# Routed experts: 48-row pieces of two tiles' down projections side by side on halves of TensorE's array, their weights fetched for each tile

## What is computed

```python
logits = jnp.einsum('ed,btd->bte', gate_w, x)
scores = jax.nn.sigmoid(logits) + gate_b
weights, indices = jax.lax.top_k(scores, TOP_K)
weights = weights / weights.sum(-1, keepdims=True)
shared_out = jax.nn.silu(x @ w1_shared) * (x @ w3_shared) @ w2_shared
...
h1 = jnp.einsum('btd,edc->btec', x, w1_routed)
h2 = jnp.einsum('btd,edc->btec', x, w3_routed)
h3 = jax.nn.silu(h1 * h2)
experts_out = jnp.einsum('btec,ecd->bted', h3, w2_routed)
routed_out = jnp.einsum('bted,bte->btd', experts_out, router_probs)
return shared_out + routed_out
```

## Time and profile before

| | |
|---|---|
| median of 3 runs | 1259.91 us (1259.74 to 1263.67) |
| the profiled execution's own time | 1262.89 us |
| its span | 1261.1 us |
| PE busy | 1217.7 us (97%), 10122 matmul records |
| PEld busy | 1072.9 us (85%) |
| DVE, ACT, POOL busy | 848.5, 602.7, 499.1 us (67, 48, 40%) |
| DMA | 111.29 MB, 88 GB/s over the span |
| chain that ended last | PE 87%, DVE 7%, issue 2%, DMA 2%, ACT 1%, POOL 1% |
| L816, PE, up projection | x316, 469 ns each |
| L833, PE, routed down projection | x316, 380 ns each |

### The profile page before, as it was taken

The page is one execution under the profiler, slowest core; times in us unless marked ns, Lnnn a source line. Parts: engine busy times, 40 slices in busy tenths (PEclk is TensorE's granted clock), DMA queues, the critical chain, the costliest instruction groups (busy, mean ns, idle before and its releaser), DMA issues.

```text
span 1261.1 us, 26966 instructions
## 1 busy us (share of the span) xinstructions
PE 1217.7 (97%) x10122; PEld 1072.9 (85%) x10122; DVE 848.5 (67%) x1706; ACT 602.7 (48%) x1353; POOL 499.1 (40%) x489
## 2 busy tenths in 40 slices
PE   5999999999998999999989999999999999999997
PEld 4788888888887777777779999999999999999996
DVE  5646776676677444344458878787886766777686
ACT  3434434433443455555545455454555545555543
POOL 2121433433424300000057767767764444444443
PEclk9999999999999999999999999999999999999999
DMA  6764325415129433333221201101110100000001
GB/s 221 287 227 160 125 74 189 156 48 185 52 77 360 157 106 105 105 102 109 80 101 30 63 26 60 34 27 59 33 61 1 34 1 1 1 2 1 1 26 43
DMA packets 62847, 111.29 MB, mean 88 GB/s; under 512 B 6912, under 2 KB 35456, under 8 KB 61184
## 3 DMA queue, kind: packets, MB, share of 16 engines
q1 hardware_dynamic: 56576, 92.77, 20.9%
q0 software_dynamic: 6144, 16.79, 4.2%
HBM read 49.37 MB, written 60.16 MB: 87 GB/s over the span
## 4 chain that ended last, share of the span: by engine, by line
PE 87%; DVE 7%; issue 2%; DMA 2%; ACT 1%; POOL 1%; SPq 0%; POOLq 0%; DVEq 0%
PE bank L816 8%; PE six L833 6%; PE bank L895 4%; PE bank L893 4%; PE bank L894 4%; PE six L934 4%; PE bank L430 4%; PE bank L432 3%; PE bank L431 3%; PE bank L971 2%; PE bank L969 2%; PE bank L970 2%; PE bank L906 2%; PE bank L905 2%; PE bank L907 2%; PE six L935 2%
## 5 line engine op out<-in xcount | busy, mean ns | idle before, releaser
L1817 DVE TENSOR_TENSOR sq<-xs 128x512 f32<-128x512 f32 x128 | 131.0, 1024 | 39.3 <-ACT xs L1312 39.3
L2037 POOL TENSOR_TENSOR rstd<-msq,half_pow 128x8 f32<-128x8 f32 x64 | 106.0, 1657 | 95.7 <-DVE msq L1824 93.9
L1293 ACT ACTIVATE pT<-six,rstd 128x256 f32<-128x256 f32 x128 | 60.8, 475 | 169.0 <-PE six L935 169.0
L2049 POOL TENSOR_TENSOR pT<-pT,tri_mul 128x512 f32<-128x512 f32 x64 | 82.0, 1281 | 142.6 <-ACT pT L1341 142.6
L816 PE MATMUL bank<-experts,xT 128*128 x316 | 109.5, 469 | 0.8 <-ACT xT L1237 0.8
L1964 POOL TENSOR_TENSOR hid_l<-hid,hid_h 128x256 fp32r<-128x256 f32 x64 | 48.4, 757 | 147.3 <-ACT hid_h L1070 147.2
L893 PE MATMUL bank<-bw_h,xT1h 128*128 128x512 f32 x256 | 105.6, 413 | 0.8 <-ACT v L1317 0.8
L1381 DVE TENSOR_TENSOR yT1l<-six,yT1h 128x512 fp32r<-128x512 f32 x64 | 44.3, 692 | 84.6 <-ACT yT1h L1346 84.6
L895 PE MATMUL bank<-bw_l,xT1h 128*128 128x512 f32 x256 | 100.3, 392 | 0.0
L894 PE MATMUL bank<-bw_h,xT1l 128*128 128x512 f32 x256 | 100.0, 390 | 0.0
L2040 POOL TENSOR_TENSOR qn<-xs,rstd 128x256 f32<-128x256 f32 x128 | 91.6, 737 | 5.0
(11 more groups left out here) (295 smaller groups left out, 3913.5 us busy)
## 6 DMA issues: line engine op xcount, KB each, us to landing
cells_scratch<-zeros SPq DMA_DIRECT2D x8, 4352.0 KB
xg<-cells_scratch SPq DMA_DIRECT2D x79, 128.0 KB, 2.1
cells_scratch<-y SPq DMA_DIRECT2D x79, 128.0 KB, 1.7
experts<-pack_experts_dram SPq DMA_DIRECT2D x16, 608.0 KB
raw<-pack_attn_dram SPq DMA_DIRECT2D x8, 1024.0 KB, 5.0
w_full<-pack_w_dram SPq DMA_DIRECT2D x2, 1024.0 KB, 10.5
out_dram<-x_all SPq DMA_DIRECT2D x8, 256.0 KB, 2.1
xT_scratch<-xT1h_c SPq DMA_DIRECT2D x7, 256.0 KB, 2.1
```

The costliest lines, as they stand in the source:

```text
L1817: dve.tensor_tensor(out=sq[:, tt, :], in0=x_qk, in1=x_qk, op=ALU.mult).then_inc(sq_sb, 1)
L2037: pool.tensor_tensor(out=rstd[:, r, :], in0=msq[:, r, :], in1=half_pow[:], op=ALU.pow).then_inc(rstd_sb, 1)
```

## The change

The down projection of a routed tile is split into 128 and 48 rows. The last 128 rows of `w2` stay in SBUF (`experts` shrinks to 960 columns for each expert). The first 48 rows come from a new input `pack_rest` by one DMA for each tile (`load_rest`, 48 x 256 numbers), to partitions 0 to 47 for an even tile and 64 to 111 for an odd one, and count on the semaphore that the tile's rows count on, now named `tile_loaded`. DVE writes an odd tile's hidden values 64 columns further right, so that after the transposes their first 48 lie on partitions 64 to 111. The transposes, their order (the 128 first) and the copy keep their sizes; the copy goes to one of four buffers, `zTr`. `routed_down` is one matmul, of two passes. `routed_rest` multiplies 48 rows on one half of the array's rows; the ones of tiles i-3 (lower half, bank 4) and i-2 (upper half, bank 5) stand together at odd i. Each adds to what `routed_down` left in its bank. On ACT the two results are copied at odd i. The shared expert keeps `shared_down`, the old form.

```diff
+ER = EW - D
+HALF, REST = P // 2, HE - P
...
-        experts = sc("experts", [P, NE, EW])
+        experts = sc("experts", [P, NE, ER])
...
+        zTr = region(XT_END, LATE)("zTr", [P, 4, 2, P])
+        rest = sc("rest", [P, GROUP // 2, D])
...
+            def load_rest(i, j):
+
+                r = HALF * (j % 2)
+                sp.dma_start(rest[r:r + REST, j // 2, :], pack_rest[bass.ds(expert_of(i), 1)].rearrange("a p d -> p (a d)"))\
+                  .then_inc(tile_loaded[j], 16)
...
                 load_rows(j, j, c[j])
+                load_rest(j, j)
...
                     store_rows(GROUP * (g - 1) + j, j, c[j])
+                    if j < count:
+                        load_rest(GROUP * g + j, j)
...
-                pe.wait_ge(xg_loaded[j], 16 * (i // GROUP + 1))
+                pe.wait_ge(tile_loaded[j], 32 * (i // GROUP + 1))
...
+            def routed_T(i, r):
+
+                pe.wait_ge(z2_sb, NS + i + 1)
+                after(pe, zT_sb, NS + i - 1)
+                for c, first in enumerate((HALF * r + REST, 0)):
+                    last = pe.transpose(six[:, 2 + r, c * P:(c + 1) * P], z2[:, r, first:first + P], ident[:])
+                last.then_inc(z2_ps, 1)
...
+            def routed_down(i, r):
+                pe.wait_ge(zT_sb, NS + i + 1)
+                after(pe, y2_sb, NS + i - 1)
+                pe.matmul(six[:, 4 + r, 0:D], zTr[:, i % 4, 0, :], weights(expert_of(i), KD * 2 * HE, D), start=True, stop=False)
+
+            def routed_rest(i, r):
+
+                rows = slice(HALF * r, HALF * r + REST)
+                pe.matmul(six[:, 4 + r, 0:D], zTr[rows, i % 4, 1, :], rest[rows, i % GROUP // 2, :],
+                          start=False, stop=True).then_inc(down2_ps, 1)
...
-                expert_down(m - 2, m % 2, expert_of(i - 2) if i >= 2 else None)
-                hidden_T(m - 1, (m - 1) % 2)
-            m = NS + NTILE
-            expert_down(m - 2, m % 2, expert_of(NTILE - 2))
-            hidden_T(m - 1, (m - 1) % 2)
-            expert_down(m - 1, (m - 1) % 2, expert_of(NTILE - 1))
+                if i < 2:
+                    shared_down(m - 2, m % 2)
+                else:
+                    routed_down(i - 2, i % 2)
+                if i >= 3 and i % 2:
+                    routed_rest(i - 3, 0)
+                    routed_rest(i - 2, 1)
+                if i == 0:
+                    hidden_T(m - 1, 1)
+                else:
+                    routed_T(i - 1, (i - 1) % 2)
+            routed_down(NTILE - 2, 1)
+            routed_rest(NTILE - 3, 0)
+            routed_rest(NTILE - 2, 1)
+            routed_T(NTILE - 1, 0)
+            routed_down(NTILE - 1, 0)
+            routed_rest(NTILE - 1, 0)
...
-                else:
+                elif i % 2:
+                    expert_out(i - 3, (i - 3) % GROUP)
                     expert_out(i - 2, (i - 2) % GROUP)
...
+            def routed_T(i, r):
+                dve.wait_ge(z2_ps, NS + i + 1)
+                dve.wait_ge(down2_ps, NS + i - 3)
+                dve.tensor_copy(zTr[:, i % 4, :, :].rearrange("p c t -> p (c t)"), six[:, 2 + r, 0:2 * P]).then_inc(zT_sb, 1)
...
-                dve.scalar_tensor_tensor(out=z2[:, r, 0:HE], in0=th2[:, r, :], scalar=1.0, in1=u2[:, r, :],
+                dve.scalar_tensor_tensor(out=z2[:, r, HALF * r:HALF * r + HE], in0=th2[:, r, :], scalar=1.0, in1=u2[:, r, :],
```

More of the change, by code:

```diff
@@ L54, with build @@
 LN_EPS, RMS_EPS = 1e-5, 1e-6
-def build(nc, x, pack_qk, pack_vo, pack_w1, pack_w3, pack_w2, pack_attn, pack_experts, pack_shared, gate_b, q_norm, k_norm,
+def build(nc, x, pack_qk, pack_vo, pack_w1, pack_w3, pack_w2, pack_attn, pack_experts, pack_rest, pack_shared, gate_b, q_norm, k_norm,
           rope_cosT, rope_sinT, ident_c, hadamard_c, stairs_c, tri_mul_c, q_row_c, k_rows_c, before_c, route_c, out):
@@ L247, in build @@
         TABLE_STEPS = 12
-        xg_loaded = [sem(f"xg_loaded{j}") for j in range(GROUP)]
+        tile_loaded = [sem(f"tile_loaded{j}") for j in range(GROUP)]
         y2_stored = [sem(f"y2_stored{j}") for j in range(GROUP)]
@@ L396, in _, with expert_of @@
             sp.wait_ge(tables_made, 1)
+            packed = nc.values_load_multi_w_load_instructions(
+                tile_pack[0:1, :], engines=[mybir.EngineType.SP], min_val=0, max_val=NE ** PACK - 1,
+                skip_runtime_bounds_check_because="four numbers of experts, each under sixteen, as base-16 digits")[1]
+            def expert_of(i):
+                return (packed[i // PACK] >> (4 * (i % PACK))) & (NE - 1)
             c = cells(0, GROUP)
@@ L825, in hidden_T, with shared_down @@
                 last.then_inc(z2_ps, 1)
-            def expert_down(m, r, e=None):
+            def routed_T(i, r):
[4 more added lines that the diff above has]
+                last.then_inc(z2_ps, 1)
+            def shared_down(m, r):
                 pe.wait_ge(zT_sb, m + 1)
@@ L831, in expert_down @@
                     first = KD * 2 * HE + c * D
-                    w = raw[:, 0, first:first + D] if e is None else weights(e, first, D)
-                    last = pe.matmul(six[:, 4 + r, 0:D], zT[:, r, c, :], w, start=c == 0, stop=c == 1)
+                    last = pe.matmul(six[:, 4 + r, 0:D], zT[:, r, c, :], raw[:, 0, first:first + D], start=c == 0, stop=c == 1)
                 last.then_inc(down2_ps, 1)
+            def routed_down(i, r):
[6 more added lines that the diff above has]
+                          start=False, stop=True).then_inc(down2_ps, 1)
             pe.wait_ge(sh_lo, 1)
@@ L852, in _ @@
                 if m >= 2:
-                    expert_down(m - 2, m % 2)
+                    shared_down(m - 2, m % 2)
                 if m == 2:
@@ L1282, in _ @@
                     unit_hi(0, 0, i - UNIT0)
+            expert_out(NTILE - 3, (NTILE - 3) % GROUP)
             expert_out(NTILE - 2, (NTILE - 2) % GROUP)
@@ L1810, in _ @@
                     unit_lo(0, 0, i - UNIT0)
-            hidden_T(NS + NTILE - 1, (NS + NTILE - 1) % 2)
+            routed_T(NTILE - 1, 0)
             def squares(n, i, tt):
@@ L2104, in _layouts, with up @@
                                     chunks(np.ascontiguousarray(wo[:, r].T)).reshape(P, -1)], 1))
[L2107 to L2112, removed]
+    def up(w1, w3):
+        return np.stack([w1, w3], 1).reshape(KD, P, 2 * HE).transpose(1, 0, 2).reshape(P, -1)
+    down = np.zeros((2 * P, D), f)
+    down[:HE] = w2s
     return dict(pack_qk=qk, pack_vo=np.concatenate(vo, 1),
@@ L2117, in _layouts @@
                 pack_w2=chunks(np.ascontiguousarray(W2.T)).reshape(P, -1),
-                pack_attn=np.stack(attn), pack_shared=expert(w1s, w3s, w2s),
-                pack_experts=np.stack([expert(w1r[e], w3r[e], w2r[e]) for e in range(NE)]))
+                pack_attn=np.stack(attn), pack_shared=np.concatenate([up(w1s, w3s), chunks(down).reshape(P, -1)], 1),
+                pack_experts=np.stack([np.concatenate([up(w1r[e], w3r[e]), w2r[e][REST:]], 1) for e in range(NE)]),
+                pack_rest=np.ascontiguousarray(w2r[:, :REST]))
 def _rotations(rope_cos, rope_sin):
```

1 line of the change is left out of this document (removed).

## The result

| | before | after |
|---|---|---|
| median | 1259.97 us (1259.74 to 1263.67, 4 runs) | 1272.89 us (1272.34 to 1274.92, 4 runs) |
| profiled execution, its span | 1262.89, 1261.1 us | 1272.66, 1270.6 us |
| PE busy | 1217.7 us | 1220.1 us |
| PEld busy | 1072.9 us | 1048.6 us |

The changed kernel takes 1.0099 times as long (95% interval 1.0077 to 1.012): slower by 12.9 us, where 11.8 were forecast (1271.7 us). The page's summary shows little of it: PE is busy for 2.4 us more, with the same number of records. The reason is visible only tile by tile.

What follows compares the result with a forecast made beforehand. A chain through the xT copy on ACT and the sequencer bounds three tiles of four, PE the rest. +12.2 - 0.4 + 0.2 + 0.4 - 0.6 = +11.8 us, median 1271.7 us, range 1265 to 1280.5.

Steps and rivals of the forecast that it cites:

- Even tiles: Routed tiles losing two of four down passes: PE's work falls 0.43 us, tile stays 2.52, gain 0.
- the chain: Routed loop: next rows' transposes, xT copy on ACT, sequencer, next up projection's weight load; 2.53 us load to load.
- Rival B: Routed stretch: the chain does not hold even tiles, which take PE's 2.06 us; total 1254.2 us, chance 0.06.
- Odd tiles: Routed tiles with two down passes plus two rests on array halves: 2.83 us, set by PE.
- The price of a switch: Changing the array's division, read from quarters: two switches cost 2 x (0.09) + 0.10 + 0.06 = 0.34 us.
- Rival A: Odd tiles: switches are free, tile needs 2.49 us, pair 5.05; total 1260.3 us, chance 0.10.
- rival C: Odd tiles: the halves do not overlap, +0.216 us x 39 = +8.4; total 1280.1 us, chance 0.10.
- The stretch: Routed loop: a pair goes from 5.03 to 5.35 us, +0.32 for 38 pairs, +12.2; longer tiles give -0.4.
- the disturbed tiles: Routed loop: about ten tiles 0.03 to 0.15 us longer than the pattern; odd tiles have room: -0.4 us.
- Tile 0, SP, ACT, DVE: Tile 0's second transfer comes later, +0.2 us (0 to 0.5); SP's third transfers, ACT and DVE copies cost 0.
- The end: Last two tiles: rests add bare switches, 0.82 and 0.95 us against 0.43 for each of three removed halves: +0.4.
- The expert weights: Loads ahead of xT1l shrink by 128 KB per expert, VectorE can't begin much earlier: -0.6 us (0 to -1.9).

Runs made afterwards that it cites:

- e1: Kernel before, with the second half of each routed down projection left out: 1258.14 us, ratio 0.9979.
- e3: Changed kernel, with the next tile's rows transposed ahead of the up projection and copied on ACT ahead of `expert_linear`: 1254.01 us, ratio 0.9934.
- e7: Kernel before, with the second half of each routed down projection left out and the next tile's rows transposed and copied early: 1232.49 us, ratio 0.971.
- e5: Changed kernel, with `load_rest` left out from tile 8 on: 1281.38 us, ratio to its own before 1.0097.
- e4: Kernel before, with the next tile's rows transposed ahead of the up projection and copied on ACT ahead of `expert_linear`: 1256.51 us, ratio 0.996.
- e2: Changed kernel, with the rests run on the whole array with weights from `experts`, so no change of division: 1275.16 us, ratio 1.0105.
- e8: e3 with four tiles' rests behind one switch, larger buffers, and SP issuing loads ahead of stores: 1255.04 us, ratio 0.9883.
- e9: The kernel of e3 run again, unchanged, on the third chip: 1262.13 us, ratio 0.9944.

## Why the prediction was right

**Even tiles: gain 0.** Right. The tile stayed at 2.52 to 2.53 us in 30 of 38 cases (2.55 to 2.68 in the others), with PE's load 0.44 behind the copy. e1, e3 and e7 show the cause: the pitch of tiles with two register operations does not move when work is taken away, and falls to PE's own work once the chain is moved. Rival B (a chain that does not hold) is out.

**Odd tiles: 2.83.** Measured 2.84. (The prediction's terms, as rounded there, add up to 2.85.) The parts fit as well: L866 to L871 takes 0.52 (0.216 + 0.31 = 0.53 forecast), L871 to L852 0.64 (0.63), L852 to L836 0.27 (0.28). The price of a switch read from quarters thus holds for halves: (2.837 - 2.054) - 2 x 0.216 = 0.35 us there and back in e3, 0.34 forecast. Rival A (switches free, pair 5.05) and rival C (halves one after the other, 0.216 more) are out: the four passes of a pair of rests, 0.48 and 0.38 us long, take 0.70 in all. The first instruction behind a change of division waits for 0.1 us in each direction: on the way there 0.52 - 2 x 0.216 = 0.09, on the way back 0.64 less the 0.32 from first to second passes and one pass of 0.216, 0.10.

**The stretch: +12.2 - 0.4.** From the first `rows_T` to the last, 78 intervals, before took 627.95 - 430.85 = 197.1 us and after 636.88 - 427.75 = 209.1, +12.0, in which the last switch is not contained; with its 0.3 it is +12.3 for the 38 pairs, where 11.8 were forecast. The pair came out at 5.363 instead of 5.35, 0.5 us over 38 pairs; the disturbed tiles gave back some 0.3. There were 16 of these before (2.55 to 2.68 us), not about ten, but their excess is the 1 us that was assumed.

**Tile 0, SP, ACT, DVE: 0.2 and 0.** e5 shows no cost of the fetches in the loop. In tile 0 the distance from the first transpose to the first up projection is 1.18 us, before 1.17; what the fetch can delay is the first transpose itself. PE's wait ahead of it is 0.34 to 0.48 us in before, e1 and e4, 0.42 in after, 0.69 in e2 and 1.28 in e3, where another 0.35 follows before tile 1; in e2 and e3 the profile names `rest` as what ended it. The 0.2 (0 to 0.5) covers after and e2. In e3 the two waits are 1.3 us longer than the one of e4, a cost of the first fetches that no other run has.

**The end: +0.4.** From the last `rows_T` to the first L894 (now L943) it is 7.54 us before and 8.14 after, +0.60, of which about 0.34 is the switch of the last odd tile. That leaves +0.26. The prediction's own terms, 0.82 + 0.95 - 3 x 0.43, make 0.48 and not 0.4. The last rows after, which answer to the earlier trace rows:

```profile
641.13 0.69 PE L866 MATMUL six<-experts,zTr 128*128 x2 [0.60 <-DVE zTr L1817]
641.76 0.70 PE L871 MATMUL six<-rest,zTr 48*128 48x256 f32 x4
...
644.06 0.70 PE L871 MATMUL six<-rest,zTr 48*128 48x256 f32 x2
```

**The expert weights: -0.6.** The size is only partly settled. PE waited for `xT1l` 1.9, 0.6 and 1.7 us in before, e1 and e4 and 0, 0.2 and 0.7 in after, e2 and e3: 1.1 less. From a mark at 330 us to the start of the routed experts the first three take 0.3 us more on average, but single traces scatter by about 0.6 either way. So the smaller loads shorten the wait, most of that is lost behind VectorE as the prediction said, and the remainder is too small to be told from nothing.

**Together.** The pairs with the disturbed tiles give +12.3, the end +0.3, tile 0 about +0.2 and the expert weights perhaps -0.3: +12.5 us against 12.9 measured and 11.8 forecast. The forecast did not hit by errors that cancel: the pairs carry nearly all of it, and they came out as worked out.

**The profiled execution.** The two spans differ by 9.5 us, not 12.9. The routed experts start at 427.75 after and at 430.85 before, 3.1 earlier. Nearly all of this is there within the first 30 us of the program, which the change does not touch. Where L489 (L509 after) first starts, before is 2.57 us behind (25.29 against 22.72). 2.0 of it come from one instruction on VectorE, ahead of the one that PE waits for. Before, then after:

```profile
21.56 3.25 DVE L1381 TENSOR_TENSOR w_l<-w_full,w_h 128x1024 fp32r<-128x1024 f32 x1
```
```profile
21.02 1.22 DVE L1432 TENSOR_TENSOR w_l<-w_full,w_h 128x1024 fp32r<-128x1024 f32 x1
```

Before, POOL had begun a long addition (`x_all`, to 27.04) at 21.39, ahead of it; after, POOL began at 21.91, behind it. PE idled for 3.15 us in before and 1.12 in after. Then came a stretch in which the trace of before has a lower clock (PEclk 0.51 where it was 1.00 in the stretch ahead), 26.4 to 29.9 us, which that of after does not have. It follows a stretch in which PE was busy for 1.11 of 3.40 us, where after it was busy for 3.28. The two stretches of before (columns as in the earlier trace rows):

```profile
23.00:26.40 3.40, 1.11 (x32) 0.89 (x32) 3.40 (x4) 0.00 (x0) 3.40 (x2) 1.00 0.07 8
26.40:29.90 3.50, 3.50 (x36) 3.04 (x36) 2.42 (x7) 2.03 (x4) 0.63 (x1) 0.51 0.00 0
```

At its end before is 3.64 us behind (29.28 against 25.64), and 2.91 at L477 (33.13 against 30.22). The prediction's sum started from this one execution and was scaled back by the 3.0 us that it lay above the median.

## What to carry to other kernels

Before work is removed from an engine that is 99% busy, look for a loop through other engines whose length happens to equal the tile's: here less work was worth 6% of itself until one operation was moved, and all of it afterwards. Work that is gathered into every second tile pays in full there and gains nothing in the other if such a loop holds that one. Where a switch has a fixed price (0.35 us there and back in e3 for two results, and no more than 0.36 in e8 for four), gather as many uses behind it as buffers allow, and check what else comes in bursts then: loads queued behind a store that waits became the next wait.

## What the runs showed of the hardware that was not expected

- The chain's length moves with the sequencer's register operations: 2.52 us with two behind the semaphore wait, 2.42 with one (e1). They are not counted as busy, and the profile calls the gap "issue" (after, 484.60 to 485.04: 0.44 us with three of them, of 36, 36 and 46 ns, PEld busy for 0.00).
- Two matmuls of two passes each on different halves, written in the program one after the other, overlap: they begin 7 ns apart and end together 0.70 us later (L871, after). Eight such passes take 1.06 us up to the transposes behind them (e8), where eight on the whole array would take 8 x 0.216 = 1.73.
- The same VectorE instruction on 128x1024 numbers takes 1.22 us with POOL idle (18.69, before; `x_all` begins at 21.39) or idle for the first 0.89 of it (21.02, after; `x_all` begins at 21.91), and 2.44 to 3.25 us while POOL's `x_all` runs (2.44 at 25.67, before, where it runs until 27.04; 3.25 at 21.56, before; 2.47 at 23.08, after). That POOL is the cause is argued from the times alone.
- On the second and the third chip the kernel before takes 9.4 us longer than on the first. e3 and e9 are one kernel on the first and the third chip. The last L509 starts at 376.35 and 376.84 us, the first up projection of a routed tile at 430.05 and 436.80, and the tiles take 2.054 and 2.837 us on both. So 6.3 us arise between. e9 has a pause there that e3 does not have, with a lower clock behind it, PEclk 0.54 (columns of the second row as in the earlier trace rows, PEclk third from the end):

```profile
422.70 1.65 PE L860 MATMUL six<-raw,zT 128*128 128x256 f32 x3 [4.13 <-issue]
```
```profile
421.00:428.00 7.00, 5.30 (x18) 4.28 (x19) 1.29 (x5) 2.17 (x6) 1.51 (x2) 0.54 0.14 48
```

All five traces from the second and the third chip (e5 to e9) have a pause of 3.5 to 5.6 us at a down projection of the shared expert between 418 and 425 us; none of e1 to e4, before and after has one. For e7 (4.82 us) and e8 (5.56) the profile names ACT's `zT` as what ended it, for the other three nothing ("issue"), and where the rest of the 9.4 us lies stays open.
